# The order of the waits in front of each TensorE call, in a fused attention and feed-forward kernel

## The reference

```
qkv = shift_token(x) @ wqkv                     # 128 -> 3 * 512, 8 heads of 64
q, k = rotary_xpos(l2norm(q) * qs, l2norm(k) * ksc)
o = softmax(mask(8 * q @ k.T)) @ v              # windows of 64: own and previous one
x = x + o @ wo
h = layernorm(shift_token(x)) * lg + lb
a, g = split(h @ w1 + b1)                       # 2 * 341 columns
x = x + (a * gelu(g)) @ w2 + b2
```

## Time and profile before

| | |
|---|---|
| median of 3 runs | 486.68 us |
| the three runs | 485.76, 486.68, 488.96 us |
| span of the profiled execution | 482.6 us |
| time of the profiled execution around its span | not recorded on its own; the median of the runs lies 4.1 us above the span |
| PE busy / idle | 448.6 / 34.0 us |
| DVE, ACT, POOL busy | 380.1, 344.1, 320.9 us |
| granted TensorE clock, mean | 0.997 of full speed |
| DMA queues | 9.1% of 16 engines' span |

### The profile page before, as it was taken

One profiled execution on the slowest core, in us unless ns is written; L12 is line 12 of the kernel. 1 busy time (PEld: TensorE's weight loads), 2 busy tenths in 40 slices (PEclk: granted clock), 3 DMA queues, 4 the chain that ended last, 5 costly groups with the idle time before them and its releaser, 6 DMA issues.

```text
span 482.6 us, 15720 instructions
## 1 busy us (share of the span) xinstructions
PE 448.6 (93%) x6288; PEld 287.2 (60%) x6288; DVE 380.1 (79%) x743; ACT 344.1 (71%) x901; POOL 320.9 (66%) x270
## 2 busy tenths in 40 slices
PE   7889999998988989998999999999998999999993
PEld 5666666556665567665555665565645655656662
DVE  4955576878898388989968888699688697878776
ACT  2156666574758898797777987886787788877832
POOL 4522260888659987999987986884978449674102
PEclk9999999999999999999999999999999999999998
DMA  6102202010001100010000101110001000101102
GB/s 184 56 4 48 85 16 49 3 23 5 3 4 23 26 1 3 2 25 1 23 3 23 23 2 23 24 24 2 23 1 25 1 22 1 25 1 24 24 1 87
DMA packets 13476, 11.42 MB, mean 24 GB/s; under 512 B 4210, under 2 KB 10716, under 8 KB 13404
## 3 DMA queue, kind: packets, MB, share of 16 engines
q1 hardware_dynamic: 13404, 10.42, 8.3%
HBM read 5.05 MB, written 1.05 MB: 13 GB/s over the span
## 4 chain that ended last, share of the span: by engine, by line
PE 58%; DVE 19%; issue 8%; ACT 8%; POOL 5%; DMA 1%; SPq 0%; POOLq 0%; DVEq 0%; ACTq 0%
PE bank L731 8%; PE bank L611 8%; PE bank L514 7%; ACT bank L1332 5%; PE bank L687 4%; PE bank L697 4%; DVE mx_a L1816 4%; PE bank L650 4%; PE bank L620 3%; PE bank L668 3%; PE bank L548 3%; PE bank L746 3%; DVE p_b L1898 2%; PE bank L631 2%; DVE rc L1872 2%
## 5 line engine op out<-in xcount | busy, mean ns | idle before, releaser
L2448 POOL TENSOR_TENSOR r_qk<-ss,minus_half 128x16 f32<-128x16 f32 x32 | 93.8, 2930 | 2.7
L2441 POOL TENSOR_TENSOR rc<-rc,rs 128x1024 f32<-128x1024 f32 x32 | 75.5, 2361 | 23.3 <-DVE rs L1878 23.2
L1332 ACT ACTIVATE bank<-bank,mn_b 128x128 f32<-128x128 f32 x256 | 88.9, 363 | 2.2 <-DVE mn_b L1886 2.2
L1816 DVE TENSOR_REDUCE mx_a<-bank 128x2 f32<-128x512 f32 (+1 forms) x96 | 61.2, 684 | 25.9 <-PE bank L525 25.4
L1285 ACT ACTIVATE pT_k<-bank 128x512 f32<-128x512 f32 x96 | 52.9, 598 | 30.8 <-PE bank L525 30.8
L2455 POOL TENSOR_TENSOR rc<-rc,r_qk 128x1024 f32<-128x1024 f32 x32 | 60.9, 1904 | 2.3
L611 PE MATMUL bank<-wqkv,xS 128*128 128x512 f32 x128 | 61.8, 605 | 0.3 <-DVE mx_a L1816 0.3
L1332 ACT ACTIVATION_READ_ACCUMULATOR bank<-bank,mn_b 128x1 f32 x256 | 58.8, 230 | 0.0
L514 PE MATMUL bank<-qT_a 32*128 32x256 f32 (+1 forms) x768 | 48.5, 341 | 2.8 <-DVE mx_a L1816 0.7
L1872 DVE TENSOR_TENSOR rc<-bank,tab_c 128x1024 f32<-128x1024 f32 x32 | 39.0, 1218 | 14.4 <-ACT sq L1307 14.0
L731 PE MATMUL bank<-yfT,w 128*128 128x512 f32 (+3 forms) x108 | 48.1, 559 | 0.4
(11 more groups left out here) (136 smaller groups left out, 873.6 us busy)
## 6 DMA issues: line engine op xcount, KB each, us to landing
v_b<-v_b SPq DMA_DIRECT2D x32, 128.0 KB, 2.3
wqkv<-in_L_ffn_wqkv_dram SPq DMA_DIRECT2D x2, 768.0 KB, 5.9
x_all<-in_L_attn_x_dram SPq DMA_DIRECT2D x1, 768.0 KB, 4.9
out_dram<-pT_k SPq DMA_DIRECT2D x3, 256.0 KB, 2.3
w<-in_L_ffn_w_dram SPq DMA_DIRECT2D x2, 341.0 KB
wo<-in_L_ffn_wo_dram SPq DMA_DIRECT2D x2, 256.0 KB, 5.9
const<-consts_dram SPq DMA_DIRECT2D x1, 352.0 KB, 6.3
x_all<-in_L_attn_x_dram SPq DMA_DIRECT2D x1, 256.0 KB, 3.0
```

The source lines that it names most:

```text
L1332: m = s.activation(x, x, ACT.Exp, bias=mn_b[:, qt, c, p:p + 1], scale=-1.0, accum_out=sum_b[:, qt, c, p:p + 1])
L1816: v.tensor_reduce(mx_a[:, qt, h0:h0 + nh], full(src).rearrange("p (h k) -> p h k", h=nh), AX.X, ALU.max).then_inc(S("a_mx"), 1)
L2441: g.tensor_tensor(rc[:, k % 2, :, :], rc[:, k % 2, :, :], rs[:, k % 2, :, :], ALU.add).then_inc(S("b_add"), 1)
L2448: g.tensor_tensor(r_qk[:, n, :], ss[:, n, :], minus_half[:, :], ALU.pow).then_inc(S("b_r"), 1)
```

## The change

Each PE helper gets a keyword argument `ends`. If it is given, its wait is issued first, ahead of the call's own waits and the frees. In the list, of the waits of a call the one that ended last in a trace is handed over as `ends`, and the others stay where they were. A call whose own first wait ended last is left as it was. No wait is added or dropped; no call, bank or transfer changes place. On DVE, `f_act` waits for `f_gate` before `f_up`.

```diff
-            def b_scores(k, pair, *free):
+            def b_scores(k, pair, *free, ends=()):
                 i, qt = k // 2, k % 2
                 qk = qkT[i % 2]
+                if ends:
+                    after(t, *ends)
                 if k == 0:
                     t.wait_ge(ld_b, 16)
                 t.wait_ge(S("b_trT_out"), k + 1)
                 for f in free:
                     after(t, *f)
...
-            def a_quad(k, u, banks, *free):
+            def a_quad(k, u, banks, *free, ends=()):
...
+                if ends:
+                    after(t, *ends)
                 for f in free:
                     after(t, *f)
                 if k < BATCH and u == 0:
...
-            def f_gated(g, c, dst, *free):
-                f_in(g, c, 1, dst, *free)
+            def f_gated(g, c, dst, *free, ends=()):
+                f_in(g, c, 1, dst, *free, ends=ends)
...
-            a_quad(1, 2, (2, 7, 0, 1), of("a_mx", 1, 1, 12), of("a_exp", 0, 1, 12))
+            a_quad(1, 2, (2, 7, 0, 1), of("a_exp", 0, 1, 12), ends=of("a_mx", 1, 1, 12))
...
-            b_turn_qk(17, 0, group("f_y", 2), batch("b_x", 6))
+            b_turn_qk(17, 0, batch("b_x", 6), ends=group("f_y", 2))
...
-            b_scores(19, 3, unit("b_pT_out", 17))
+            b_scores(19, 3, ends=unit("b_pT_out", 17))
...
+                v.wait_ge(S("f_gate"), g * NCH + c + 1)
                 v.wait_ge(S("f_up"), g * NCH + c + 1)
-                v.wait_ge(S("f_gate"), g * NCH + c + 1)
                 after(v, *chunk("f_down", prior(g), c))
                 v.scalar_tensor_tensor(out=act[0:n, c, own], in0=full(src)[0:n, 0:nb * SEQ],
```

More of the change, by code:

```diff
@@ L466, in a_turn_k, with a_turn_q @@
                 m.then_inc(S("a_stk"), 1)
-            def a_turn_q(b, pair, *free):
+            def a_turn_q(b, pair, *free, ends=()):
+                if ends:
+                    after(t, *ends)
                 t.wait_ge(S("a_qk"), b + 1)
@@ L536, in a_turn_m, with a_values @@
                 m.then_inc(S("a_mT"), 1)
-            def a_values(b, g, dst, *free):
+            def a_values(b, g, dst, *free, ends=()):
+                if ends:
+                    after(t, *ends)
                 t.wait_ge(S("a_exp"), b * NX + 2 * pair_k(b, 2 if g < 2 else 5) + g % 2 + 1)
@@ L551, in a_values, with a_turn_back @@
                 m.then_inc(S("a_pv"), 1)
-            def a_turn_back(b, pair, *free):
+            def a_turn_back(b, pair, *free, ends=()):
+                if ends:
+                    after(t, *ends)
                 t.wait_ge(S("a_ov"), b * 2 + 2)
@@ L600, in b_input, with b_proj @@
                     t.wait_ge(S("f_x"), (i - BATCH) // 2 + 1)
-            def b_proj(k, pair, *free):
+            def b_proj(k, pair, *free, ends=()):
                 i, n = k // 2, k % 2
                 l = i // BATCH
+                if ends:
+                    after(t, *ends)
                 if k % (BATCH * TILES) == 0:
@@ L659, in b_scores, with b_turn_p @@
                 m.then_inc(S("b_sc"), 1)
-            def b_turn_p(k, pair, *free):
+            def b_turn_p(k, pair, *free, ends=()):
+                if ends:
+                    after(t, *ends)
                 t.wait_ge(S("b_p"), k + 1)
@@ L670, in b_turn_p, with b_values @@
                 m.then_inc(S("b_pT"), 1)
-            def b_values(k, pair, *free):
+            def b_values(k, pair, *free, ends=()):
                 i, qt = k // 2, k % 2
+                if ends:
+                    after(t, *ends)
                 t.wait_ge(S("b_pT_out"), k + 1)
@@ L1010, in _ @@
-            b_turn_qk(11, 3, chunk("f_act", 0, 2), group("f_yT", 1))
+            b_proj(13, 1, ends=unit("b_pT_out", 9))
+            b_turn_qk(11, 3, chunk("f_act", 0, 2), ends=group("f_yT", 1))
             f_gated(1, 0, 0, unit("b_o", 9))
             f_gated(1, 1, 1, chunk("f_gate", 0, 2))
-            f_down(0, 0, 6, unit("b_trT_out", 11))
+            f_down(0, 0, 6, ends=unit("b_trT_out", 11))
             f_down(0, 1, 6)
             f_down(0, 2, 6)
-            b_proj(14, 1, unit("b_rot", 13))
+            b_proj(14, 1, ends=unit("b_rot", 13))
@@ L1051, in _ @@
[L1051 to L1057 removed]
+            b_proj(19, 3, unit("b_o", 13), ends=chunk("f_gate", 1, 2))
+            b_v(15, 2, ends=chunk("f_act", 1, 1))
+            b_turn_qk(17, 0, batch("b_x", 6), ends=group("f_y", 2))
@@ L1215, in _ @@
             f_norm_t(8, 1)
-            f_down(6, 0, 2, batch("b_x", 15))
+            f_down(6, 0, 2, ends=batch("b_x", 15))
             f_down(6, 1, 2)
```

601 lines of the change are left out of this document (313 added, 288 removed).

## The result

The changed kernel takes 484.15 us (median of 22 runs, 483.69 to 485.81); the kernel before, run beside it, takes 486.65 us (median of 22). The ratio is 0.9958, with a 95% interval of 0.9939 to 0.9976: some 2.05 us less (the two medians lie 2.5 us apart). The forecast was 485.3 us and 1.4 us less. Run again beside other kernels, the changed one gave 0.994 (0.991 to 0.9969) and 0.9957 (0.9926 to 0.9988).

What follows compares the result with a forecast made beforehand. The prediction took PE's order of work as the bound, with PE idle 34.0 of 482.6 us. Savings of 1.3 and 0.2 us less 0.1 on DVE made 1.4 off 486.68: 485.3 us, range 482.8 to 487.6.

Steps and rivals of the forecast that it cites:

- The wait that the source has first rides on the load: At PE calls and `f_act`: the first wait in source sits on the weight load or operation, others become separate steps.
- All 17 hops: On the chain into PE: 16 hops of 0.13 or 0.14 us and `b_proj(0)` at 0.25 should fall to 0.04.
- 0.08 us a call: At a stalled PE call: moving the late wait onto the weight load saves 0.08 us, between 0.06 and 0.10.
- The hops of the chain are worth 1.5 us, and are the ceiling: Chain into PE: 16 x 0.08 plus 0.2 for `b_proj(0)` gives 1.5 us; whatever happens off the chain can't add.
- `f_act` loses 0.1 us: On DVE: with `f_up` as a separate step, the one `f_act` on the chain released by PE loses 0.1 us.
- The median stands 4.1 us above the span and carries over: Whole kernel: the median before, 486.68 us, is 4.1 above the profiled span of 482.6; the same gap holds after.
- The first, that all 64 stalled calls count: On PE: the sequencer runs ahead, so 64 x 0.08 = 5.1 us go, giving 481.6 us; chance 0.12.
- The second rival: Whole kernel: source order or chosen waits don't matter, so 486.7 us, or a second path limits the gain; chance 0.16.
- The third, DVE: `f_act` on DVE: most of 27 operations lose 0.1 us each on the path, 2.7 us, giving 488.0; chance 0.06.

Runs made afterwards that it cites:

- the 17 calls: Kernel before with the late wait put first only in the 16 counted chain calls and `b_proj(0)`, `f_act` as before: 486.27 us, ratio 0.9984.
- the two half kernels: Kernel before with the late wait first in 17 counted calls alone (ratio 0.9984), or in all other changed calls (0.9977); `f_act` as before in both.
- the filler: Changed kernel plus six matmuls of unused result ahead of `a_out(3)`, where PE stands idle: 483.97 us, ratio 0.9951.
- the shorter waits: Changed kernel with `f_act` as before, duplicate PE waits dropped, a few more late waits first on PE and POOL: 483.4 us, ratio 0.9957.
- the last kernel with the filler: Changed kernel with `f_act` as before, duplicate waits dropped, some waits reordered, six unused matmuls ahead of `a_out(3)`; run again: 482.84 us, ratio 0.9927.

## Why the prediction was right in the time and wrong in a step

**The wait that the source has first rides on the load: right.** All 17 hops went to 0.04, the steps moved from line 322 to the own waits with 429 in all, and with the order reversed the chain has 31 hops of 0.14.

**0.08 us a call: right.** From the last release to the first weight load, before had 76 calls with 0.10 behind a separate step and 42 with at most 0.05; the changed kernel has 10 and 107. Of the ten left, seven have the late wait twice, so that one copy is always separate. In the trace of the 17 calls the single steps are 0.05 to 0.09 us, 0.07 on average, and 0.17 at `b_proj(0)`.

**The hops of the chain are worth 1.5 us, and are the ceiling: the step that failed.** It failed twice, in opposite senses, and that the forecast of 1.4 us came near the 2 that were measured is partly luck. First, the sum was too high for the calls that it counts: they gave 0.66 us where 1.3 were forecast for the same stretches, since 0.4 of the 1.1 that they save is given back at later waits. Second, it left out calls that gave 1.48 us. The sum took only the hops into PE behind DVE or ACT. The chain of before shows others, between one PE call and the next. Around 63:

```profile
62.19 0.79 PE bank L548 x16
62.98 0.12 issue
63.10 1.15 PE bank L514 x16
```

The weight load there had waited for ACT's `pT_k` for 0.36 us, but PE's last matmul ended later than ACT, so the chain goes on along PE. Behind 20 us it has seven such pieces of 0.09 to 0.12 us (at 50.44, 62.98, 65.21, 75.28, 397.26, 403.84 and 443.53), 0.73 together; in the changed kernel the longest left is 0.05. They were there to be counted. Beyond them the chain passes over stalls on PE altogether. Before, in the chain and in the timeline around 34.9:

```profile
34.69 0.18 PE bank L525 x16
34.87 0.02 issue
34.90 1.17 PE bank L514 x32
```

```profile
34.62 0.25 PE L525 MATMUL bank<-const 32*32 32x64 bf16 x16
34.87 1.01 PEld L514 LDWEIGHTS bank<-qT_a 32*128 32x128 f32 x32
34.90 1.17 PE L514 MATMUL bank<-qT_a 32*128 32x128 f32 x32
```

The chain shows PE followed by PE, 0.02 us apart, as if nothing had been waited for. In the changed kernel:

```profile
34.59 0.25 PE L535 MATMUL bank<-const 32*32 32x64 bf16 x16
34.77 0.98 PEld L524 LDWEIGHTS bank<-qT_a 32*128 32x128 f32 x32
34.77 1.17 PE L524 MATMUL bank<-qT_a 32*128 32x128 f32 x32
```

From the first small matmul to the first large one it is 0.28 us before and 0.18 now: a tenth saved in a place where the chain shows no hop at all. The modelled ends of the matmuls had covered the wait. How the 1.48 us divide between the pieces on the chain and those that it doesn't show, I haven't worked out. My criterion for a wrong ceiling, a span more than 2 us shorter with the hops as forecast, would not have caught it: the span fell by 0.7. It took the two half kernels to see it. PE's idle time was to fall by 1 to 2 us with its busy time the same; it fell by 2.2, and the busy time rose by 1.5 with the dip.

**`f_act` loses 0.1 us: right.** By the calls it is 0.1 to 0.2. On the chain it stands once, with 0.08 instead of 0.03. Its step is not recorded at the line of `f_up`, as I had written, except for group 0 (3 times): from group 1 on it shares a step with the `f_down` wait and shows at line 322.

**The median stands 4.1 us above the span and carries over: right by luck.** In the runs that carry both figures the time is 1.75 to 3.0 us above its own span, for these two kernels 1.9 to 2.0 in every one. The rest of the 4.1 was spread: the profiled execution of before was one of its short ones (484.2 to 484.9 us, clock 0.997). So the pair of spans compares a kernel without a dip with one that has it. Taken alike, the gain is 1.93 us by the calls outside the dip and 1.5 us by the lowest runs of each (484.18 of 106, 482.70 of 46), and 2.05 by the ratio.

**The rivals.** The first, that all 64 stalled calls count with 5.1 us, had part of the truth: calls off the forecast's list do count, at 1.48 us. Its size is excluded by the intervals (4.4 us less at most), and its mechanism finds no support: reordered waits that were over gave 1.0003, and 475 more steps left a ratio of 0.9939. The rule that I had put beside it, of the Trainium skill, "Perfetto Trace Analysis", section "Sequencer Loop", has the sequencer push an engine instruction into a queue, where it waits for its semaphores. The runs agree with it in so far as steps that are over cost nothing from 190 us on, behind matmuls still in the queue. The second rival, no effect, is excluded by the intervals of three ratios, 0.9988 at most. The third, DVE, cost 0.1 to 0.2 and not 2.7.

## What to carry to other kernels

Where several waits stand in front of one instruction, put the one that ends last first: here it saved 0.06 to 0.10 us a stalled call, and the order of waits that were over made no difference that could be measured. Don't take the chain's hops behind other engines as a ceiling for a change that touches many calls: count its issue between two calls of the same engine too, and expect stalls that it doesn't show. Halves of the change, run by themselves, tell more than the view, and comparing the start of each call in two traces resolves tenths of a microsecond that the times don't, as long as the trace is repeated: one of them held a stall of 1.1 us that had nothing to do with the edit. When one of two spans holds a dip of the clock, compare the calls outside it.

## What the runs showed of the hardware that was not expected

The clock of TensorE fell to the lower of its two levels behind an idle stretch of 1.72 us, and the kernel lost 1.3 us by it. The stretch is there in all eleven profiles without the filler, before and changed kernel included, at 1.47 to 1.72 us; in eight the clock fell behind it, for 3.4 us (6.8 in one). Its length doesn't decide: behind 1.47 us (the kernel with more steps) and 1.54 us (the 17 calls) the clock fell, behind 1.53 us (before, and the waits that were over) and 1.61 us (the shorter waits) it didn't. So it isn't shown that the changed kernel dips because it waits longer. With the filler, which leaves 0.26 to 0.36 us of idle time, the clock didn't fall there in any of three profiles (one of them has a dip at 179 us, behind an idle stretch of 1.1 us, one at 7.5 us). Eight of eleven against none of three speaks for the idle stretch as the cause, and isn't proof.

Whether the changed kernel dips more often than the one before is open too. In the runs of which the mean clock is known, 36 of 106 of the kernel before have 0.996 or more, but only 1 of 46 of the changed kernel. But the mean also holds a fall of the clock at the very end that lasts 5 to 9 us in these profiles: 0.994 stands on one with the dip in the middle (the changed kernel's first) and on one without (the last kernel with the filler). Nor is the clock all of the spread: 14 of the changed kernel's 46 runs lie at 485.2 to 485.9 us, 1.5 above the group at 483.4 to 484.3, with clocks of 0.988 to 0.997. The stall at 61.8 us in the kernel of waits that were over, in a run of 485.75 us, has that size. What makes the first 26 us come out up to 3 us later in some executions is open.
